# Low-rank attention: a head's softmax totals in a bank of the row scores, ahead of its last value products, and inverted in one operation

## The reference, cut to what matters

```python
c_q = h_t @ W_DQ + b_DQ                       # (8, 1024, 32)
c_kv = h_t @ W_DKV + b_DKV
q = concat(heads of c_q @ W_UQ + b_UQ, heads of c_q @ W_QR + b_QR)      # 8 heads of 128 + 32
k = concat(heads of c_kv @ W_UK + b_UK, h_t @ W_KR + b_KR)
v = heads of c_kv @ W_UV + b_UV
scores = einsum('bhsd,bhtd->bhst', q, k) * scale
attn = softmax(scores, axis=-1)
o = einsum('bhst,bhtd->bhsd', attn, v)
x = x + (o @ W_O + b_O)
```

## Time and profile before

| | |
|---|---|
| Median of 3 runs | 1882.62 us (1881.56 to 1885.85) |
| The profiled execution: its own time | 1882.77 us |
| its span, first to last instruction | 1881.0 us |
| PE busy | 1737.6 us, 92% |
| DVE busy | 1366.7 us, 73% |
| ACT busy | 1111.9 us, 59% |
| POOL busy | 1176.7 us, 63% |
| L1926, the inversions | 128 of 128x128, 120.4 us, mean 942 ns |
| L1816, row maxima | 1024, 663.1 us, mean 675 ns |

### The profile page before, as it was taken

The page is one execution under the profiler, slowest core; times in us unless marked ns, Lnnn a source line. Parts: engine busy times, 40 slices in busy tenths (PEclk is TensorE's granted clock), DMA queues, the critical chain, the costliest instruction groups (busy, mean ns, idle before and its releaser), DMA issues.

```text
span 1881.0 us, 40394 instructions
## 1 busy us (share of the span) xinstructions
PE 1737.6 (92%) x15489; PEld 1266.4 (67%) x15489; DVE 1366.7 (73%) x3039; ACT 1111.9 (59%) x2102; POOL 1176.7 (63%) x907
## 2 busy tenths in 40 slices
PE   4589999999868999999999999999999999999995
PEld 4468888888756566666666666666666666676664
DVE  5557777766685877787778778778777877877862
ACT  5456666676574565665566566565655656655552
POOL 4300111100274597888798888888888888888892
PEclk9789999999897999999999999999999999999998
DMA  4656566663000000000001000000001000000101
GB/s 120 157 131 151 147 151 155 147 157 82 27 1 1 2 9 7 10 7 9 7 9 20 6 10 18 10 7 20 8 7 21 7 9 7 18 10 7 21 9 30
DMA packets 198614, 81.56 MB, mean 43 GB/s; under 512 B 152552, under 2 KB 177428, under 8 KB 198292
## 3 DMA queue, kind: packets, MB, share of 16 engines
q1 hardware_dynamic: 198420, 78.98, 18.8%
HBM read 39.83 MB, written 29.88 MB: 37 GB/s over the span
## 4 chain that ended last, share of the span: by engine, by line
PE 46%; DVE 17%; issue 4%; ACT 1%; POOL 0%; DMA 0%; SPq 0%; POOLq 0%; DVEq 0%; ACTq 0%
PE pair L1904 13%; PE pair L1808 10%; DVE amax L1816 8%; PE pair L1863 7%; PE pair L1859 7%; DVE o_inv L1926 5%; PE pair L1915 3%; DVE q_low L1749 2%; PE pair L1641 2%; PE pair L1682 1%; PE pair L1632 1%; PE pair L1668 1%; DVE stats L486 1%; PE pair L1655 1%; DVE mv L494 0%
## 5 line engine op out<-in xcount | busy, mean ns | idle before, releaser
L1874 ACT ACTIVATE prob<-pair 128x512 f32<-128x512 f32 x1024 | 603.9, 597 | 468.0 <-PE pair L1863 412.7
L1816 DVE TENSOR_REDUCE amax<-pair 128x1 f32<-128x512 f32 x1024 | 663.1, 675 | 252.2 <-PE pair L1808 250.0
L1808 PE MATMUL pair<-key_hl,q_hi 128*128 128x512 f32 x1024 | 446.1, 438 | 23.5 <-DVE amax L1816 19.5
L1863 PE MATMUL pair<-q_low,key_h 65*128 65x512 f32 x1024 | 407.2, 398 | 0.0
L1859 PE MATMUL pair<-q_hi,key_hl 128*128 128x512 f32 x1024 | 406.2, 397 | 0.4 <-ACT prob L1874 0.4
L1888 POOL TENSOR_TENSOR w_mix<-w_mix,prob 128x1024 f32<-128x1024 f32 x160 | 381.9, 2387 | 27.6 <-ACT prob L1874 10.8
L1888 POOL TENSOR_TENSOR Wm<-Wm,prob 128x1024 f32<-128x1024 f32 x155 | 369.3, 2383 | 21.7 <-ACT prob L1874 5.5
L521 POOL TENSOR_SCALAR veps<-mv 128x8 f32<-128x8 f32 x47 | 11.4, 242 | 473.7 <-DVE mv L494 472.8
L1808 PEld LDWEIGHTS pair<-key_hl,q_hi 128*128 128x128 f32 x1024 | 196.4, 192 | 141.1 <-issue 54.9
L1904 PE MATMUL pair<-prob,values 128*32 128x256 f32 x4096 | 251.5, 387 | 5.5 <-DVE o_norm L1933 5.5
L1177 DVE TENSOR_REDUCE mx_neg<-pair 128x4 f32<-128x512 f32 x256 | 164.9, 687 | 100.1 <-PE pair L1081 100.1
(11 more groups left out here) (208 smaller groups left out, 2364.5 us busy)
## 6 DMA issues: line engine op xcount, KB each, us to landing
rows_mem<-once SPq DMA_DIRECT2D x128, 128.0 KB, 2.0
queries<-rows_mem SPq DMA_DIRECT2D x64, 256.0 KB, 4.8
keys<-rows_mem SPq DMA_DIRECT2D x16, 1024.0 KB, 7.1
rows_mem<-once SPq DMA_DIRECT2D x128, 64.0 KB, 1.9
q_low<-shift_cols SPq DMA_DIRECT2D x512, 0.5 KB, 2.0
yT<-o_norm SPq DMA_DIRECT2D x256, 32.0 KB, 1.9
x<-x_dram SPq DMA_DIRECT2D x8, 512.0 KB, 7.4
out_dram<-x SPq DMA_DIRECT2D x7, 512.0 KB, 3.4
```

Of the source, the lines that this page charges most:

```text
L1808: e.matmul(bank(ROW_BANKS[n % 3]), q_hi[:, k, t * P:(t + 1) * P], key_hl[:, b % 2, i * HALF:(i + 1) * HALF], start=True, stop=True, skip_g ...
L1816: e.tensor_reduce(amax1[:, u % 2, t, i:i + 1], bank(ROW_BANKS[(2 * r + i) % 3]), AX_X, ALU.max).then_inc(*row_maxed.up((r, i)))
L1863: e.matmul(bank(j), key_h1[:, b % 2, ks], q_low[:, k, sl], start=False, stop=True, skip_group_check=True).then_inc(*key_scored.up((g, half)))
L1874: e.activation(prob1[:, g % P_BUFS, half * HALF:(half + 1) * HALF], bank(K_BANKS[(2 * g + half) % 3]), ACT.Exp, scale=SCALE1).then_inc(*ke ...
```

## The change

The totals of head u move ahead of the value products of its last four tiles, in the same step, 8u + 11. They go to the bank whose turn it is among the three of the row scores: a list `row_uses`, in PE's order, holds two uses for the row scores of each step and one for the totals of each head, and each use takes bank 4, 5 or 6 by its place in this list. A use waits for what the use three places before leaves: a row maximum, or the inversion of a head's totals. The inversion is now one operation of 256 columns, in step 8u + 11 of DVE, behind that step's row maxima; the multiplication comes in step 8u + 12, ahead of its maxima, and waits for the value products as well. `ones_col`, the operands and the counts of the matmuls are as before.

```diff
+        row_uses = []
+        for g, early, late in plan_m:
+            if 0 <= g + ROW_LEAD < total:
+                row_uses += [("row", g + ROW_LEAD, i) for i in range(2)]
+            if g % NT == 3 and 0 <= g // NT - 1 < B * NH:
+                row_uses.append(("total", g // NT - 1, 0))
+        row_place = {use: i for i, use in enumerate(row_uses)}
+
+        def row_bank(use):
+            return bank(ROW_BANKS[row_place[use] % 3])
+
+        def row_bank_free(e, use):
+            if row_place[use] >= 3:
+                kind, a, i = row_uses[row_place[use] - 3]
+                e.wait_ge(*(row_maxed.at((a, i)) if kind == "row" else o_inverse.at(a)))
...
-            n = 2 * r + i
-            if n >= 3:
-                e.wait_ge(*row_maxed.at(divmod(n - 3, 2)))
-            e.matmul(bank(ROW_BANKS[n % 3]), q_hi[:, k, t * P:(t + 1) * P], key_hl[:, b % 2, i * HALF:(i + 1) * HALF],
+            row_bank_free(e, ("row", r, i))
+            e.matmul(row_bank(("row", r, i)), q_hi[:, k, t * P:(t + 1) * P], key_hl[:, b % 2, i * HALF:(i + 1) * HALF],
...
             e.wait_ge(*key_exp.at((4 * n + 3, 1)))
+            if n % 2 == 1:
+                if u < B * NH - 1:
+                    e.wait_ge(*summed_keys.at(NT * u + 6))
+                    parts = prob1[:, (NT * u + 7) % P_BUFS, :], key_sum[u % 2]
+                else:
+                    parts = [prob1[:, t, :] for t in range(NT)]
+                row_bank_free(e, ("total", u, 0))
+                for n_part, part in enumerate(parts):
+                    for q in range(4):
+                        done = e.matmul(row_bank(("total", u, 0))[q * DC:(q + 1) * DC, 0:QUARTER], ones_col[:, :],
+                                       part[:, q * QUARTER:(q + 1) * QUARTER], start=n_part == 0,
+                                       stop=n_part == len(parts) - 1, skip_group_check=True)
+                done.then_inc(*totalled.up(u))
             for g in range(4 * n, 4 * n + 4):
...
-            if n % 2 == 1:
-                if u < B * NH - 1:
-                    e.wait_ge(*summed_keys.at(NT * u + 6))
-                    parts = prob1[:, (NT * u + 7) % P_BUFS, :], key_sum[u % 2]
-                else:
-                    parts = [prob1[:, t, :] for t in range(NT)]
-                for n_part, part in enumerate(parts):
-                    for q in range(4):
-                        ins = e.matmul(bank(PVB)[q * DC:(q + 1) * DC, QUARTER:2 * QUARTER], ones_col[:, :],
-                                       part[:, q * QUARTER:(q + 1) * QUARTER], start=n_part == 0,
-                                       stop=n_part == len(parts) - 1, skip_group_check=True)
             ins.then_inc(*pv_done.up(n))
...
-        def dve_invert_totals(e, u, i):
-            sl = slice(i * P, (i + 1) * P)
-            e.wait_ge(*pv_done.at(2 * u + 1))
+        def dve_invert_totals(e, u):
+            e.wait_ge(*totalled.at(u))
             if u >= 2:
                 e.wait_ge(*o_ready.at(u - 2))
-            e.reciprocal(o_inv[:, u % 2, sl], bank(PVB)[:, QUARTER + i * P:QUARTER + (i + 1) * P]).then_inc(
-                *o_inverse.up((u, i)))
+            e.reciprocal(o_inv[:, u % 2, :], row_bank(("total", u, 0))[:, 0:QUARTER]).then_inc(*o_inverse.up(u))
 
         def dve_normalise(e, u):
-            e.wait_ge(*o_inverse.at((u, 1)))
+            e.wait_ge(*o_inverse.at(u))
+            e.wait_ge(*pv_done.at(2 * u + 1))
...
-                u, t = divmod(g - 13, NT)
-                if t == 0 and 0 <= u < B * NH:
-                    dve_invert_totals(e, u, 0)
+                u, t = divmod(g - 11, NT)
                 if t == 1 and 0 <= u < B * NH:
-                    dve_invert_totals(e, u, 1)
-                if t == 2 and 0 <= u < B * NH:
                     dve_normalise(e, u)
...
+                if t == 0 and 0 <= u < B * NH:
+                    dve_invert_totals(e, u)
```

More of the change, by code:

```diff
@@ L1480, in build_program @@
         half_added = signal("half_bias_added")
+        totalled = signal("totals")
         o_inverse, o_ready = signal("weighed_inverse"), signal("weighed_normalised")
@@ L1815, in dve_row_max @@
                 e.wait_ge(*row_topped.at((u - 2, t // 4)))
-            e.tensor_reduce(amax1[:, u % 2, t, i:i + 1], bank(ROW_BANKS[(2 * r + i) % 3]), AX_X, ALU.max).then_inc(
+            e.tensor_reduce(amax1[:, u % 2, t, i:i + 1], row_bank(("row", r, i)), AX_X, ALU.max).then_inc(
                 *row_maxed.up((r, i)))
```

## The result

| | before | after |
|---|---|---|
| Median of the runs | 1883.04 us (1881.56 to 1885.85, 4 runs) | 1858.86 us (1854.77 to 1861.51, 4 runs) |
| Profiled execution: its own time, span | 1882.77, 1881.0 us | 1859.78, 1858.0 us |

The ratio after to before is 0.9868 (95% interval 0.9846 to 0.9890): 24 us faster, where 39 were forecast. The same kernel run again later gave 1859.18 us and 0.9874 (0.9851 to 0.9896). Of all runs in this document one execution, of the third experiment, was in a slower state of the chip at a lower granted clock (2042.71 us, 0.927), and it counts in no figure.

The account below looks back on a forecast made before the run. DVE was taken to set PE's pace in odd halves. Gains of 4.1 us (first sequence), 27.8 (six middle), 5.4 (last) and 1.8 (tail) made 39.1, so 1882.77 became 1843.7 us; range 1835 to 1862.

Parts of the forecast that it names:

- What bounds the kernel: Odd halves of each head: PE waits 1.08 us for DVE's inversions and multiplication, while DVE idles 2.94 us earlier.
- The odd half: After the block's start, inversion (1.75 us) and multiplication fit under PE's work; 1.8 us of DVE leave the late stretch.
- statistics: Odd half with four statistics, 11.14 us before, DVE busy without a gap: gain taken as 0.5 us, between 0.2 and 1.1.
- No item: Odd half without side item, where ACT normalises rows: 1.08 us over the even half, gain taken as 1.0.
- The rival on the clock: PE's 1.2 GHz dips, in four of eight sequences: ended by denser work, 1837; one in each sequence, 1850. Chance 0.08.
- Queued behind the new wait of DVE: Odd half: only DVE work later than 2.8 us after block start queues there, except early `cq`, `key_hl` or four statistics.
- That is the tightest head of a sequence: Sequence 4: POOL's sum ended 1.6 us before the block's start, taken as the least slack of a sequence.
- 1.6 us and more to spare in every later head: Argument against totals becoming a wait for POOL: its sums end at least 1.6 us early in every later head.
- named signs of being wrong: Inversions starting behind value products, row scores waiting for `o_inv`, or L1915 waiting for POOL in heads 8 and later.
- T + 3.95: Statistics half, T the start of totals and value products: when inversion, four statistics and multiplication would be done on DVE.
- Totals wait for row maxima: Rival: totals wait for a row maximum each time, 0.3 us a head: 1863. Chance 0.09, shared with partly waiting for POOL.
- The slower case by POOL: Rival: POOL's sums come 1.5 us late in all 64 heads, so PE waits 96 us: 1940. Chance of slower 0.03.

Follow-up runs that it names:

- Run 1: Changed kernel, but the inversion again two operations of 128 columns back to back in the new place: 1858.64 us, 0.9872 to the kernel before.
- run 2: Changed kernel, but totals issued behind the value products again, still in a row-score bank with one inversion: 1928.0 us, 1.024 to the kernel before.
- run 3: Changed kernel, but DVE inverts two steps later, so totals hold a row-score bank for two steps: 2016.69 us, 1.0725 to the kernel before.
- run 9: Changed kernel, but ACT's normalisation spread over four steps, two tiles each, instead of four tiles in two steps: 1855.85 us, 0.9848 to the kernel before.
- run 4: Changed kernel, but the quantisation scale and two steps behind it run one step later, when POOL has no sum: 1849.54 us, 0.9832 to the kernel before.
- run 8: Changed kernel, but in heads 0 and 62 alone the value products come first again, the inversion waiting for them: 1856.12 us, 0.9853 to the kernel before.
- run 6: Changed kernel, but the scale computed in its old step with two SBUF operands, adding a lower-bound tile: 1872.0 us, 0.9927 to the kernel before.
- run 7: Changed kernel plus one unused tile of 4 bytes a partition, never read or written: 1870.73 us, 0.9942 to the kernel before.

## Why the prediction was right or wrong

**What bounds the kernel: right.** The maxima and inversions lost most of their share of the chain, and all odd halves together got 32 us shorter. Run 1 shows that the one operation has no part in it, run 2 that without the order the rest of the change is a loss, run 3 that the totals can't be left in a row bank for two steps.

**The odd half: right in mechanism, several sizes off.** Halves of the fourth sequence, gain forecast and measured, us: L1641 0.34, 0.33; L1648 0.66, 0.63; L1655 0.79, 0.77; plain 1.08, 1.07; statistics 0.5, 0.67. The last sequence's two came to 1.17 and 1.71, where 1.1 and 1.6 were taken. Three terms were too large:
- "No item: 1.08; ACT normalises rows there, so I take 1.0": 0.43. I named ACT and then priced it at 0.08; with PE no longer waiting for DVE, ACT's four tiles are the next bound (run 9). 3.4 us in six halves.
- L1668: 0.34 taken, 0.13 measured, and L1665 0.8 taken, 0.64 measured: 2.2 us in twelve. What holds them was not tried by itself; it is not the scale step, since run 4 leaves them as they are. In the half with L1665, PE's wait of 0.3 us for ACT's `q_hi` stands in both traces, as the prediction said.
- L1679/L1682: "I take 0.2", measured 0.13 without a dip (11.50 to 11.37). The −0.6 of the ledger is 0.9 of such gain less one dip more (6 against 5). The rival on the clock came true neither way: denser work did not end the dips, nor did each sequence get one. Its count was also one short: one of its four places, from 884.26 to 891.09 us, holds two dips.

**No term for the even halves: this step failed.** The prediction adds up what odd halves give back and takes the even ones as they were. Its list of what moves ("Queued behind the new wait of DVE for the totals are only things that DVE did later … except early side work") is of the odd half, and it names `cq`, `key_hl` and the statistics, not the quantised product. The scale step stands near the start of an even half. Its 0.7 us was in the trace before, and 128x32 elements should have looked far too little for it; I didn't ask what it waited for. DVE came to it 0.65 us earlier, it grew to 2 us, and the six even halves took 3.9 us more; with the long wait gone, 3.7 came back (run 4).

**"That is the tightest head of a sequence": this step failed in the last one.** The slack was read in the fourth sequence. POOL adds a bias there too (at 1199.86, run 8), but ahead of a head whose sums end 5.5 us early; in the last sequence the bias falls right ahead of head 62's sums. "1.6 us and more to spare in every later head" was false in the trace before, where head 62 had 0.82. Head 0 cost 1.5 us, as forecast; head 62 cost 1.8 that nobody had forecast. It is also one of the named signs of being wrong, L1915 waiting for POOL in a head from 8 on, come true in that one head.

**The stretch in front: chance.** In the ten other profiles of kernels with the same tiles the first value products start between 638.5 and 644.3 us; before at 638.5, after at 642.1. The range of 1838 to 1850 for the forecast had no room for this: it was wide for the unseen prices and left out what untouched code does from run to run. The wider range, 1835 to 1862, held the result in good part by luck: its upper end stood for totals that wait for maxima or for POOL, and of the 16 us that were missing only the 1.8 of head 62 are of that kind.

**Two readings of rows.** The half of 9.82 us that was set against a plain one of 7.88 (1244.61 to 1254.43) holds ACT's normalisation and is not plain; the plain odd halves before took 9.83, so the 1.08 stands by luck. In the statistics half T + 3.95 is less than its terms, 2.80 + 0.86 + 0.41 = 4.07; by them 0.1 us would be left and not 0.2.

**The rivals.** "Totals wait for row maxima" did not show: in the odd blocks after, PE's totals wait for nothing but POOL in those two heads. The slower case by POOL did not come, since its slack held in 62 heads. A slower case exists all the same, at a place where I hadn't looked for one: the inversion behind the value products, with a row bank in DVE's hands meanwhile (run 2).

## What to carry to other kernels

When an engine that is late gets idle time filled, list every operation that moves in time, and for each one that takes longer than its elements explain, ask what it waited for: that wait has another length at another moment. Read slack against a helper engine in each kind of block, the first and the last above all, and take the block behind a removed wait to be bound by the engine next in line at its full work, not by PE. Where two kernels differ in a tile, compare a stretch of untouched code before believing the totals.

## What the runs showed of the hardware

- A DVE operation on 128x32 elements in SBUF takes 0.18 us with POOL idle and up to 2.15 us when a POOL sum of 1024 columns runs (2.19 us in run 6, with two operands in SBUF); it ends 0.04 to 0.05 us behind the sum. The maximum over 512 columns in SBUF (L1522) took its 0.67 us inside a POOL sum, so not every operation of DVE waits.
- One unused tile of four bytes a partition cost 12 us (run 7), with the DMA share of the windowed attention up from 0.60 to 0.72 at the same bytes.
- TensorE's granted clock dipped to the 1.2 GHz level in stretches in which PE was busy all the time; one dip cost 1.55 us (run 4).
- Time of an inversion out of PSUM: 128 columns 0.94 us, 256 columns 1.76 us, as two of 128 back to back (1.77). Run 1 shows no saving by merging.
